# Key transfers spread over half cells, and probabilities of two cells added on GpSimd before the ones product, in a four-sublayer fp32 block on one core

## The chip, the core and the metric

One core of a Trainium2 chip runs the whole program: TensorE (PE) for matmuls, VectorE (DVE), ScalarE (ACT), GpSimd (POOL), and SyncE (SP), which issues nearly all DMAs. Each engine works through its own list in order and waits on semaphores. The metric is the device time of one execution in microseconds (us).

## What is computed

2048 tokens of width 128 pass six residual sublayers. All but the last but one are finished or nearly finished before the stage that matters here; that one is causal attention with 16 heads, softmax and a Gelu:

```
def _L1_attn_ref(x, Wk, bk, Wv, bv, Wf, bf):   # D_MODEL = 128, N_HEADS = 16, D_HIDDEN = 512
    Q = _split_heads(x, H)
    K = _split_heads(x @ Wk + bk, H)
    V = _split_heads(x @ Wv + bv, H)
    causal = jnp.tril(jnp.ones((S, S), dtype=bool))
    mask = jnp.where(causal, 0.0, -jnp.inf).astype(x.dtype)
    scores = jnp.einsum('bhqd,bhkd->bhqk', Q, K) + mask
    attn = jax.nn.softmax(scores, axis=-1)
    o = jnp.einsum('bhqk,bhkd->bhqd', attn, V)
    o = o.transpose(0, 2, 1, 3).reshape(B, S, -1)
    return x + jax.nn.gelu(o, approximate=False) @ Wf + bf
...
x = L0_attn_src                                # (1, 2048, 128)
x = x + 0.5 * _L0_ffn_ref(_layernorm(x, axis=-1), ...)      # 4-bit quantised
x = x + _L0_attn_ref(_layernorm(x, axis=-1), ...)           # linear attention
x = x + 0.5 * _L0_ffn_ref(_layernorm(x, axis=-1), ...)
x = x + 0.5 * _L1_ffn_ref(_layernorm(x, axis=-1), ...)      # relu
x = x + _L1_attn_ref(_layernorm(x, axis=-1), ...)           # the causal stage
x = x + 0.5 * _L1_ffn_ref(_layernorm(x, axis=-1), ...)
```

## The kernel before, in words

One list, PLAN, gives the order of all steps, and `follow` lets every engine walk it and emit its own part of each step. So the order in the plan is the order on each engine. The causal stage is built by `causal`.

Queries are cut into 4 chunks of 512, heads into 4 sets of 4 (two pairs of heads, pp = 0 and 1): 16 groups g, with chunk g // 4. A cell (g, kb) is one block of 128 keys against the 512 queries of the group's chunk; a group of chunk c has 4(c+1) cells, the last four on the diagonal and so narrower: 160 cells, numbered u. Group 8 begins with cell 48, group 12 with cell 96, group 15 with cell 144. A cell has two half cells i = 0, 1, one for each pair of heads. In half cell 0 of cell u PE makes `scores` of the first pair of heads (L1652), mostly one matmul pair `max` of a later group's row maxima (L1617), and `values` of cell u-1 (L1676: probabilities times V); in half cell 1 the other `scores`, another `max`, and `sums` of cell u-1 (L1691: a matrix of ones times the probabilities, which gives the softmax denominators). The remaining steps of a cell (transposes, output projection `wf`, the relu sublayer's `d_hidden`, `d_out`, keys and values of later chunks) stand behind the values, or, the second half of them, behind the sums.

ACT turns scores into probabilities `pr` (L966), a ring of 3 buffers of one cell each. DVE reduces each max matmul (L1289). Scores, max matmuls and most other PE outputs rotate through three PSUM sets in plan order, so a scores matmul reuses the set of the max matmul two before it, and a max matmul that of the scores in the half cell before. `row_max` (L1299 to L1303, three DVE instructions) gathers a group's maxima and splits them into two bf16 parts; PE turns them (`turn_max`, L1635), ACT copies them (L974), SP stores them into two rows of the queries (L653), where the group's first scores need them.

The denominators of a finished group go: ACT copy `take_d` (L987), gather by SP (L662), reciprocal on DVE (`invert`, L1307, two cells after the group's end), store (L669), spread to all rows (L676), product with the output on GpSimd (`norm`, L802, four cells after).

Keys and queries reach the tensors KK and QS through DRAM: GpSimd splits them into three bf16 parts (`split`, L792 to L795), SP stores these (`store_parts`, L626) and then issues 12 loads of 8 rows into KK (L634) and 12 into QS (L644), 64 KB each, one after the other. For chunk c these stand two groups before its first group, at the end of that group's maxima. `e_norm` and `d_norm` are layer norms' last step (L1088, DVE), after GpSimd's power (`rstd`, L696).

## Time and profile before

| | |
|---|---|
| median of 3 runs | 1105.21 us (1094.06 to 1112.79) |
| profiled execution | 1099.85 us |
| its span, first to last instruction | 1098.0 us |
| causal cells, from the first scores to the last exponential | 438 to 1067 us |
| mean granted TensorE clock | 0.944 of full speed |

A span is what the trace covers; what lies around it is 1.85 us. Each engine's busy time counts its instructions alone. A row of the timeline has start, duration, engine, line, operation, out<-in and count, and in brackets how long the engine had been idle and what released it. PE is TensorE, DVE VectorE, ACT ScalarE, POOL GpSimd, SPq the queue of SyncE.

### The profile page before, as it was taken

The page shows a single profiled execution, that of the slowest core. Times are in us where ns is not written, and L with a number is a line of the kernel's source. Part 1 is how long each engine was busy: PE and PEld are TensorE (multiplying, and loading weights), DVE is VectorE, ACT ScalarE, POOL GpSimd, SP SyncE. Part 2 cuts the span into 40 slices and gives each one's busy share as a digit, 9 for nine tenths or more (in the row PEclk, how much of TensorE's full clock was granted, in tenths as well). Part 3 has the DMA queues.
Part 4 walks back from the last instruction along what each step waited for, and adds up shares of the span by engine and source line. Part 5 has one row for each costly group of instructions (what it writes and reads, how often), then busy time and mean ns, then how long its engine had stood idle before and what let it go on. Part 6 is the DMA issues. An engine that isn't in the chain of part 4 may idle for free.

```text
span 1098.0 us, 19966 instructions
## 1 busy us (share of the span) xinstructions
PE 909.0 (83%) x7332; PEld 452.2 (41%) x7353; DVE 708.6 (65%) x1675; ACT 511.9 (47%) x884; POOL 257.4 (23%) x405
## 2 busy tenths in 40 slices
PE   2678887788888767928889699899899989999986
PEld 1444445666676655404334333243322223332225
DVE  7899953367887765638655487665579747677003
ACT  1133333243444323513565455656456656666763
POOL 1545420044555644204221001112000000000000
PEclk9899998898999987968999899899999989999998
DMA  5200000000000040050001400000400000000000
...
DMA packets 30935, 23.20 MB, mean 21 GB/s; under 512 B 9609, under 2 KB 27897, under 8 KB 30840
## 3 DMA queue, kind: packets, MB, share of 16 engines
...
q8 instruction: 61, 1.00, 0.4%
q10 hardware_dynamic: 912, 0.54, 0.2%
...
## 4 chain that ended last, share of the span: by engine, by line
PE 55%; DVE 18%; ACT 6%; POOL 6%; issue 6%; DMA 4%; SPq 4%; ACTq 0%; DVEq 0%; POOLq 0%
PE psum L1676 10%; PE psum L1691 10%; PE psum L1652 6%; PE psum L1617 5%; DVE arena L1289 4%; PE psum L1564 3%; PE psum L1533 2%; ACT arena L966 2%; POOL rs L696 2%; PE psum L1575 2%; DMA arena<-arena 2%; PE psum L1411 2%; PE psum L1370 2%; PE psum L1598 2%; PE psum L1705 2%
## 5 line engine op out<-in xcount | busy, mean ns | idle before, releaser
L1289 DVE TENSOR_REDUCE arena<-psum 128x2 f32<-128x1024 f32 (+2 forms) x320 | 335.6, 1063 | 154.1 <-PE psum L1617 95.7
L966 ACT ACTIVATE arena<-psum 128x1024 f32<-128x1024 f32 (+3 forms) x320 | 286.5, 897 | 157.1 <-PE psum L1652 90.7
L696 POOL TENSOR_TENSOR rs<-ve,mhalf 128x1 f32<-128x1 f32 x128 | 70.8, 559 | 397.1 <-DVE ve L1083 396.8
L1676 PE MATMUL psum<-arena 128*32 128x512 f32 (+3 forms) x1280 | 153.9, 554 | 1.3 <-ACT arena L966 1.3
L1691 PE MATMUL psum<-arena,ones 128*32 128x512 f32 (+3 forms) x1280 | 154.4, 555 | 0.0
L1617 PE MATMUL psum<-arena 48*128 48x512 bf16 (+3 forms) x640 | 113.5, 359 | 48.3 <-DMA arena<-scr_parts 20.6
L1652 PE MATMUL psum<-arena 50*128 50x512 bf16 (+3 forms) x640 | 116.9, 361 | 9.5 <-ACT arena L966 4.5
L1652 PEld LDWEIGHTS psum<-arena 50*128 50x128 bf16 x640 | 31.3, 93 | 203.8 <-issue 137.9
L802 POOL TENSOR_TENSOR arena<-arena 128x512 f32<-128x512 f32 x15 | 19.1, 1276 | 212.0 <-DMA arena<-scr_sums 212.0
L935 ACT ACTIVATE rh<-psum,fb 128x128 f32<-128x128 f32 x128 | 36.4, 369 | 66.1 <-PE psum L1564 63.2
L1617 PEld LDWEIGHTS psum<-arena 48*128 48x128 bf16 x640 | 35.9, 94 | 65.2 <-issue 26.2
L1370 PE MATMUL psum<-WguT,xqT 128*128 128x352 f32 x128 | 50.4, 522 | 7.7 <-DVE hb L1114 6.8
L1564 PE MATMUL psum<-xdT,fW 128*128 128x128 f32 x256 | 40.7, 309 | 16.4 <-DVE arena L1289 13.3
L1564 PEld LDWEIGHTS psum<-xdT,fW 128*128 128x128 f32 x256 | 35.7, 215 | 27.0 <-issue 22.5
L700 POOL TENSOR_TENSOR xv<-xv,xm 128x128 f32<-128x128 f32 x32 | 20.2, 631 | 112.4 <-DVE xv L1041 112.4
L1676 PEld LDWEIGHTS psum<-arena 128*32 128x32 f32 x1280 | 25.4, 109 | 40.8 <-issue 35.6
L1337 PE MATMUL psum<-bias_rows,onesb 128*128 128x128 bf16 (+1 forms) x107 | 28.5, 266 | 12.6 <-ACT arena L995 4.3
L854 ACT ACTIVATE th<-psum 128x352 f32<-128x352 f32 x32 | 14.8, 463 | 51.0 <-PE psum L1370 50.9
L1461 PE MATMUL psum<-arena 128*128 128x256 f32 x128 | 38.2, 397 | 0.0
L1575 PE MATMUL psum<-fW,rh 128*128 128x128 f32 x256 | 37.2, 291 | 0.0
L700 POOL TENSOR_TENSOR hv<-hv,hm 128x352 f32<-128x352 f32 x32 | 29.7, 930 | 29.8 <-DVE hv L1041 29.8
L1691 PEld LDWEIGHTS psum<-arena,ones 128*32 128x32 f32 x1280 | 25.5, 109 | 26.1 <-issue 21.4
...
## 6 DMA issues: line engine op xcount, KB each, us to landing
...
```

Source lines behind the costliest of these rows:

```text
L696: v.tensor_tensor(rs[:, u, t:t + 1], ve[:, u, t:t + 1], mhalf[:, :], ALU.pow).then_inc(s_rstd[u], 1)
L700: k = me.did(v.tensor_tensor(x, x, m, ALU.subtract))
L966: v.activation(pr[:, u % RING, pp, :, 0:CH - off], both(("scores", n))[0][:, :, off:CH], ACT.Exp).then_inc(s_p, 1)
L1289: v.tensor_reduce(MXP[:, j, 2 * pp:2 * pp + 2, m], both(("max", g, pp, j, m))[0][:, :, 0:hi - lo], AX_X, ALU.max).then_inc(s_mxd, 1)
L1370: last = mm(bank(b + k)[:, 0:GI], xqT[:, n % 2, :], WguT[:, k, :], start=True, stop=True)
L1461: last = mm(o, Wq[:, P * j:P * j + P], XNT[:, GRP * g:GRP * g + GRP], start=False, stop=True, skip_group_check=True)
L1564: last = mm(bank(b)[:, P * j:P * j + P], fW1[:, P * j:P * j + P], xdT[:, n % 2, :], start=True, stop=True)
L1575: last = mm(bank(b)[:, P:2 * P], rh[:, n % 2, j, :], fW2[:, j, :], start=False, stop=(j == FJ - 1), skip_group_check=True)
L1617: last = mm(o[:, par, 0:w], QS[c % 2][r, hp, P * j:P * j + P], KK[m][r, hp, 0:w], start=True, stop=(m < c), skip_group_check=True)
L1652: last = mm(o[:, par, off:CH], KK[kb // TPC][r, hp, P * (kb % TPC):P * (kb % TPC) + P], QS[c % 2][r, hp, off:CH], start=True, stop=(kb < T ...
L1676: last = mm(bank(O_BANK)[VD * h:VD * h + VD, off:CH], V[kb // TPC][:, kb % TPC, GH * (g % GPC) + h, :], pr[:, u % RING, h // 2, h % 2, 0:C ...
L1691: last = mm(bank(D_BANK)[VD * h:VD * h + VD, off:CH], ones1[:, 0:VD], pr[:, u % RING, h // 2, h % 2, 0:CH - off], start=(kb == 0), stop=en ...
```

## The change

In chunks 2 and 3 the full (not diagonal) cells of a group are taken in pairs (a, a+1), 40 pairs in all. GpSimd adds the probabilities of a+1 into those of a, in four instructions of 128 x 2 x 256 (`add_probs`: two halves of the queries, two pairs of heads), placed two and three cells after a. The ones product then runs over the sum, 256 queries at a time, in cells a+4 and a+5. The ring has 5 buffers (even cells use three, odd ones two), and exponentials wait for the products or additions that free theirs. The ones products of other cells stay one cell behind.

The 24 row loads of a chunk are issued two per half cell, queries and keys and the two row halves by turns, each pair once a given number of score matmuls is done. Chunk 1's store moves from half cell 10 to half cell 4. Reciprocals and norms come one cell later, Gelu one cell later and group by group, with the group outputs in a ring of 6. Maxima of groups 9 to 15 end one cell earlier. `e_norm` and `d_norm` of the causal stage and the two splitting instructions of `row_max` move from DVE to GpSimd. Some tensors of early stages now share their memory with the denominators.

```
-NORM_AT, GELU_AT = 4, 7
+PAIRED_FROM = 2
+ADD_AT, SUM_AT = 2, 4
+INVERT_AT, NORM_AT, GELU_AT = 3, 5, 8
+HELD = 6
+HALF = 256
...
-MAX_LEADS = {1: 2, 2: 3, 3: 3, 4: 3}
+MAX_LEADS = {1: 2, 2: 3, 3: 3, 4: 3, **{g: 5 for g in range(9, 16)}}
...
-        RING = 3
+        RING = 5
         pr = ce([RING, GP, 2, CH])
-        GT = [ce([GPC, CH]), ce([GPC, CH])]
-        DN = [ce([CH]), ce([CH])]
+        GT = ce([HELD, CH])
...
+        PAIRED = [a for g in range(MGROUPS) if g // GPC >= PAIRED_FROM
+                  for a in range(GROUP_U[g], GROUP_U[g + 1] - TPC, 2)]
+        SUMS = sorted([(a + SUM_AT + half, a, half) for a in PAIRED for half in range(2)]
+                      + [(a + 1, a, None) for a in range(len(CELLS))
+                         if a not in PAIRED and a - 1 not in PAIRED])
+        SUM_N = {(a, half): n for n, (_, a, half) in enumerate(SUMS)}
+        FIRST_SUM = {CELLS[a][0]: (a, half) for _, a, half in reversed(SUMS)}
+        LAST_SUM = {CELLS[a][0]: (a, half) for _, a, half in SUMS}
...
+        def slot(u):
+            return u // 2 % 3 if u % 2 == 0 else 3 + u // 2 % 2
...
-                if g % GPC == GPC - 2 and g + 2 < MGROUPS:
-                    slots[max_end[g]] += [("store_parts", g // GPC + 1), ("load_queries", g // GPC + 1)]
+            load_slot = {1: SECOND_KEYS_START + 4 * SECOND_KEYS_EVERY + 1, 2: max_end[6], 3: max_end[10]}
+            for c, first in load_slot.items():
+                slots.setdefault(first, []).append(("store_parts", c))
+                for k in range(4 * COMBOS):
+                    slots.setdefault(first + 1 + k // 2, []).append(("load_rows", c, k, first + 1 + k // 2))
...
-                    put(end + 2, "invert", g)
-                    put(end + 2, "store_inverse", g)
-                    put(end + 3, "spread_inverse", g)
+                    put(end + INVERT_AT, "invert", g)
+                    put(end + INVERT_AT, "store_inverse", g)
+                    put(end + INVERT_AT + 1, "spread_inverse", g)
                     put(end + NORM_AT, "norm", g)
...
+            for n, a in enumerate(PAIRED):
+                for k in range(2 * GP):
+                    put(a + ADD_AT + k // GP, "add_probs", 2 * GP * n + k)
...
+                    for when, a, half in SUMS:
+                        if (i, u) == (1, when):
+                            out.append(("sums", a, half))
+                            if LAST_SUM[CELLS[a][0]] == (a, half):
+                                out.append(("take_d", CELLS[a][0]))
...
+        POOL_NORMS = {x for x in PLAN[main:] if x[0] in ("d_norm", "e_norm")}
...
+            def load_rows(c, k, after):
+                par, n, keys = k % 2, k // 4, k // 2 % 2
+                if k == 0:
+                    sp.wait_ge(s_ptd, 48 * (c + 1))
+                    sp.wait_ge(s_att, c + 1)
+                    if c >= 2:
+                        sp.wait_ge(s_st, GP * GROUP_U[GPC * (c - 1)])
+                if after > 0:
+                    sp.wait_ge(s_st, after)
+                rows = slice(64 * par + QD * n, 64 * par + QD * n + QD)
+                part = scr[K_PART[n], 1] if keys else scr[Q_PART[n], 0]
+                src = part.rearrange("(a b r) s -> b r a s", b=2, r=QD)[par, :, :, CH * c:CH * c + CH]
+                if keys:
+                    sp.dma_start(KK[c][rows, :, :], src).then_inc(s_kk[c], 16)
+                else:
+                    sp.dma_start(QS[c % 2][rows, :, :], src).then_inc(s_qs[c % 2], 16)
...
+            def add_probs(n):
+                a, half, pp = PAIRED[n // (2 * GP)], n // GP % 2, n % GP
+                q = slice(HALF * half, HALF * half + HALF)
+                into = pr[:, slot(a), pp, :, q]
+                pool.wait_ge(s_av, a + 1)
+                pool.wait_ge(s_p, GP * (a + 1) + pp + 1)
+                v.tensor_tensor(into, into, pr[:, slot(a + 1), pp, :, q], ALU.add).then_inc(s_ps, 1)
+            def normed(u, n, t, y):
+                pool.wait_ge(s_rstd[u], n)
+                return v.tensor_scalar(y, X[:, t, :], mv[:, u, t, 0:1], rs[:, u, t:t + 1], ALU.subtract, ALU.mult)
+            def d_norm(n):
+                if ("d_norm", n) in POOL_NORMS:
+                    pool.wait_ge(s_xdt, n - TILES - 1)
+                    normed(4, n - TILES + 1, tile(n), xd[:, n % 2, :]).then_inc(s_xd, 1)
+            def row_max_parts(g):
+                pool.wait_ge(s_mxr, g + 1)
+                k = me.did(v.tensor_copy(MXH, MXS[:, :, :, 0]))
+                me.wait(k)
+                v.tensor_tensor(MXS[:, :, :, 1], MXS[:, :, :, 0], MXH, ALU.subtract).then_inc(s_mxn, 1)
...
-                if u >= RING:
-                    act.wait_ge(s_dn, u - RING + 1)
-                v.activation(pr[:, u % RING, pp, :, 0:CH - off], both(("scores", n))[0][:, :, off:CH], ACT.Exp
+                old = u - (4 if u % 2 else 6)
+                if old in PAIRED:
+                    act.wait_ge(s_dn, SUM_N[old, 1] + 1)
+                elif old - 1 in PAIRED:
+                    act.wait_ge(s_ps, 2 * GP * (PAIRED.index(old - 1) + 1))
+                    act.wait_ge(s_av, old + 1)
+                elif old >= 0:
+                    act.wait_ge(s_dn, SUM_N[old, None] + 1)
+                v.activation(pr[:, slot(u), pp, :, 0:CH - off], both(("scores", n))[0][:, :, off:CH], ACT.Exp
...
-                k = me.did(v.tensor_reduce(MXS[:, :, :, 0], MXP[:, :, :, 0:c + 1], AX_X, ALU.max, negate=True))
-                me.wait(k)
-                k = me.did(v.tensor_copy(MXH, MXS[:, :, :, 0]))
-                me.wait(k)
-                v.tensor_tensor(MXS[:, :, :, 1], MXS[:, :, :, 0], MXH, ALU.subtract).then_inc(s_mxn, 1)
+                v.tensor_reduce(MXS[:, :, :, 0], MXP[:, :, :, 0:c + 1], AX_X, ALU.max, negate=True).then_inc(s_mxr, 1)
...
-            def sums(u):
+            def sums(u, half):
                 g, kb = CELLS[u]
-                c = g // GPC
-                off = P * max(kb - TPC * c, 0)
-                end = kb == TPC * (c + 1) - 1
-                if kb == 0:
+                off = P * max(kb - TPC * (g // GPC), 0)
+                lo, hi = (off, CH) if half is None else (HALF * half, HALF * half + HALF)
+                first, end = FIRST_SUM[g] == (u, half), LAST_SUM[g] == (u, half)
+                if first:
                     B[D_BANK].free(pe)
+                if half is None:
+                    pe.wait_ge(s_p, GP * (u + 1))
+                else:
+                    pe.wait_ge(s_ps, 2 * GP * PAIRED.index(u) + GP * (half + 1))
                 for h in range(GH):
-                    last = mm(bank(D_BANK)[VD * h:VD * h + VD, off:CH], ones1[:, 0:VD],
-                              pr[:, u % RING, h // 2, h % 2, 0:CH - off], start=(kb == 0), stop=end,
+                    last = mm(bank(D_BANK)[VD * h:VD * h + VD, lo:hi], ones1[:, 0:VD],
+                              pr[:, slot(u), h // 2, h % 2, lo - off:hi - off], start=first, stop=end,
                               skip_group_check=True)
                 last.then_inc(s_dn, 1)
```

How this lies on the engines. PE early in group 13 (before), two half cells: scores, maxima, values, then scores, maxima (with a mask) and the sums of 512 columns.

```order
L1652 MATMUL psum<-arena 128x512 x2
L1617 MATMUL psum<-arena 128x512 x2
L1676 MATMUL psum<-arena 32x512 x4
L1652 MATMUL psum<-arena 128x512 x2
L1617 MATMUL psum<-arena 128x384 x2
L1623 MATMUL psum<-ident,mask_kq 128x64 x4
L1691 MATMUL psum<-arena,ones 32x512 x4
```

The same place of the kernel after: L1723 are the scores, L1688 the maxima, L1747 the values, L1408 and L1646 the relu sublayer's `d_out`, L1694 a mask, L1766 the sums.

```order
L1723 MATMUL psum<-arena 128x512 x2
L1688 MATMUL psum<-arena 128x512 x2
L1747 MATMUL psum<-arena 32x512 x4
L1408 MATMUL psum<-bias_rows,onesb 128x128
L1646 MATMUL psum<-fW,rh 128x128 x4
L1723 MATMUL psum<-arena 128x512 x2
L1688 MATMUL psum<-arena 128x128 x2
L1694 MATMUL psum<-ident,mask_kq 128x64 x4
L1766 MATMUL psum<-arena,ones 32x256 x4
L1723 MATMUL psum<-arena 128x512 x2
```

The sums have 256 columns in place of 512; in the group's cells 1 to 3 none stand, in its diagonal cells one more than before.

SP around chunk 3's reload (before): L626 stores, L634 and L644 are the loads, L662 gathers, L653 stores maxima.

```order
L653 DMA arena<-arena 2x512 x4
L626 DMA scr_parts<-arena 128x2x512 x3
L634 DMA arena<-scr_parts 8x8x512 x12
L644 DMA arena<-scr_parts 8x8x512 x12
L683 DMA out_dram<-X 128x128 x2
L662 DMA arena<-arena 32x1x16 x4
L669 DMA scr_sums<-arena 128x16
L676 DMA arena<-scr_sums 32x512 x4
```

The first load of chunk 1 and what follows it on SP (after): L659 stores, L676 and L678 load keys and queries, L696 gathers, L687 stores maxima, L703 and L710 store and spread the inverse.

```order
L687 DMA arena<-arena 2x512 x8
L659 DMA scr_parts<-arena 128x2x512 x3
L678 DMA arena<-scr_parts 8x8x512 x2
L676 DMA arena<-scr_parts 8x8x512 x2
L678 DMA arena<-scr_parts 8x8x512 x2
L676 DMA arena<-scr_parts 8x8x512 x2
L696 DMA arena<-early 32x1x16 x4
L678 DMA arena<-scr_parts 8x8x512 x2
L687 DMA arena<-arena 2x512 x4
...
L703 DMA scr_sums<-arena 128x16
L678 DMA arena<-scr_parts 8x8x512 x2
L710 DMA early<-scr_sums 32x512 x4
```

Gathers, stores of maxima and the inverse's two transfers now stand between the loads, and the loads of keys and queries alternate.

GpSimd near the end of the stage (after), where before nothing but L802 (here L864) and powers stood: L842 are the additions, L855 and L857 the two splitting instructions of the row maxima.

```order
L842 TENSOR_TENSOR arena<-arena 128x2x256 x12
L864 TENSOR_TENSOR arena<-arena,early 128x512
L842 TENSOR_TENSOR arena<-arena 128x2x256 x4
L855 CAST arena<-arena 128x16
L857 TENSOR_TENSOR arena<-arena 128x16
L842 TENSOR_TENSOR arena<-arena 128x2x256 x12
```

The splitting of a group's maxima waits behind the additions that stand ahead of it.

## Rows read from the trace of the kernel before

**Rows 1.** The page's first part: busy us, share of the span, instructions
```profile
PE 909.0 (83%) x7332; PEld 452.2 (41%) x7353; DVE 708.6 (65%) x1675; ACT 511.9 (47%) x884; POOL 257.4 (23%) x405
```

**Rows 2.** Windows of the three reloads: columns in the first row
```profile
core 0: us, PE busy (x) PEld busy (x) DVE busy (x) ACT busy (x) POOL busy (x), PEclk, DMA share, GB/s
472.00:492.00 20.00, 0.00 (x0) 0.00 (x0) 2.04 (x6) 0.88 (x2) 0.00 (x0) 0.56 0.54 66
606.00:626.00 20.00, 13.42 (x138) 5.50 (x134) 8.00 (x12) 9.70 (x15) 0.55 (x1) 0.96 0.54 83
773.00:790.00 17.00, 14.74 (x154) 5.65 (x146) 9.72 (x13) 10.08 (x16) 0.55 (x1) 1.00 0.52 103
```

**Rows 3.** Timeline of SP around chunk 1's store: start, us, line, operation
```profile
450.70 2.42 SPq L653 DMA_DIRECT2D arena<-arena  x4
...
464.34 1.46 SPq L626 DMA_DIRECT2D scr_parts<-arena  x3
468.07 4.17 SPq L634 DMA_DIRECT2D arena<-scr_parts  x12
```

**Rows 4.** Timeline of PE over the first stall
```profile
471.34 0.22 PE L1659 MATMUL psum<-ident,mask_qk 64*128 64x64 bf16 x4
...
492.19 0.71 PE L1617 MATMUL psum<-arena 48*128 48x512 bf16 x4 [20.63 <-DMA arena<-scr_parts]
```

**Rows 5.** Timeline over the second stall: SP's gather, the reciprocal, PE
```profile
614.96 3.69 SPq L662 DMA_DIRECT2D arena<-arena  x4
...
627.52 0.25 DVE L1307 RECIPROCAL arena<-arena 128x16 f32<-128x16 f32 x1 [10.55 <-DMA arena<-arena]
...
628.73 2.05 PE L1564 MATMUL psum<-xdT,fW 128*128 128x128 f32 x8 [8.69 <-DVE arena L1289]
...
634.18 0.84 PE L1617 MATMUL psum<-arena 48*128 48x512 bf16 x4
```

**Rows 6.** Timeline of PE after the third stall
```profile
792.96 2.05 PE L1564 MATMUL psum<-xdT,fW 128*128 128x128 f32 x8 [4.63 <-DVE arena L1289]
```

**Rows 7.** Timeline of PE over one cell of group 12
```profile
880.25 0.39 PE L1652 MATMUL psum<-arena 50*128 50x512 bf16 x2
...
880.48 0.38 PE L1617 MATMUL psum<-arena 48*128 48x512 bf16 x2
...
880.79 1.06 PE L1676 MATMUL psum<-arena 128*32 128x512 f32 x8
...
881.79 0.39 PE L1652 MATMUL psum<-arena 50*128 50x512 bf16 x2
...
883.32 0.39 PE L1652 MATMUL psum<-arena 50*128 50x512 bf16 x2
```

**Rows 8.** Timeline of PE and ACT where a half cell is short
```profile
924.85 0.39 PE L1652 MATMUL psum<-arena 50*128 50x512 bf16 x2
...
925.28 1.02 ACT L966 ACTIVATE arena<-psum 128x1024 f32<-128x1024 f32 x1 [0.61 <-PE psum L1652]
...
926.45 0.39 PE L1617 MATMUL psum<-arena 48*128 48x512 bf16 x2 [0.31 <-ACT arena L966]
```

**Rows 9.** Timeline of PE in group 15, two score matmuls
```profile
1034.23 0.39 PE L1652 MATMUL psum<-arena 50*128 50x512 bf16 x2
...
1035.55 0.39 PE L1652 MATMUL psum<-arena 50*128 50x512 bf16 x2
```

**Rows 10.** Timeline of PE: a ones product of 256 columns on a diagonal cell
```profile
530.81 0.64 PE L1691 MATMUL psum<-arena,ones 128*32 128x256 f32 x8
531.38 0.39 PE L1652 MATMUL psum<-arena 50*128 50x512 bf16 x2
```

**Rows 11.** Line L802, GpSimd's product: duration ns min/median/max, first and last start
```profile
L802 POOL TENSOR_TENSOR arena<-arena x15: 1256/1272/1327, 495.8 to 1038.4; 128x512 f32<-128x512 f32 x15
```

**Rows 12.** Waits from 438 to 690: us in total, times, longest
```profile
PE psum L1617 <- DVE arena L1289: 6.7, 13, 1.6
```

89 lines of the change are left out of this document (44 added, 45 removed).

## Prediction

> **What bounds the kernel now.** I read the page's engine totals first [rows 1]: PE is busy 83% of the span, DVE 65%, GpSimd (POOL) 23%. An average over stages says little, so I then followed the score matmuls (L1652) and exponentials (L966) cell by cell along the timeline, from 438 us, where the causal stage begins, to its end at 1068. Everything before is untouched by the edits. Two pictures come out.
>
> In undisturbed cells PE is never idle. The reader should see four blocks that repeat [rows 7]: scores 880.25, row-maximum scores 880.48, values 880.79, the next scores 881.79, and after the ones product (sums) the next cell's scores at 883.32. That is 3.07 us a cell: twice (0.54 of scores and maxima + 0.99 of values or sums). Group 15 has no maxima left to make; there a half cell takes 1.32 [rows 9], so 2.64 a cell.
>
> Between them lie stalls. The largest: PE's last matmul before 471.6, the next at 492.19, waiting 20.63 for the reload of keys and queries [rows 4]. A second: PE waits 8.69 to 628.73, because DVE's reciprocal of the denominators (L1307) sat 10.55 waiting for its gather, which SP could issue only after 24 row loads (614.96 to 618.65) and which then queued behind them; DVE's maxima, and PE with them, stood behind that reciprocal [rows 5]. A third of the same kind: 4.63 to 792.96 [rows 6]. The remaining idle times of several us are the Gelu blocks on ACT, which the change leaves where they are, one cell later.
>
> **Spreading the row loads.** Chunk 1. Now its store is issued at 464.34, behind the maxima of group 2, and the loads run from 468.07 to 492.2, 24.1 us for 24 [rows 3, 4]. After, it stands right behind the maxima of group 1, issued by 453.12 (450.70 + 2.42). With the same 3.73 from store to first load, the loads start at 456.9 and end at 480.9, if the queue works at the same rate; the issue gates (score matmuls 5 to 16) open before that, since the 16th is passed at about 469. PE arrives at 471.6, so it waits 9.3 instead of 20.6: 11.3 saved. Bounds: the chunk-3 loads move 103 GB/s against 66 here [rows 2]; at that rate they end near 472 and about 18 are saved. The last pair now stands behind the spread of group 0's inverse on SP, which can cost 3: 8 saved. I take 11.5.
>
> Chunk 2. The gather is now issued after 16 to 20 loads and the reciprocal one cell later, so I expect the 8.69 to go. But the queue was busy throughout 606 to 626 [rows 2], so the last load still lands near 626.5. The first maximum that needs it stands 5.4 behind the end of the present stall (628.73 to 634.18 [rows 5], at the low clock); PE would be there at about 620.0 + 4.5 = 624.5 and wait 2. That leaves 6.7, plus about 2 because less runs at the low clock: in [rows 2] the granted clock is 0.56 in the stall without any matmul. I take 8.5, between 5 (the wait moves) and 11.5. Chunk 3: the first user is four cells later, nothing new waits; 4.6 plus some 2.4 of low clock, 7 (4.6 to 8).
>
> What the row loads are limited by is a matter of its own: the DMA share is 0.54, 0.54 and 0.52 while they run [rows 2], about half of the 16 engines, whatever PE does. The Trainium skill (DMA: Bandwidth & Descriptors, the section on why a DMA adds 16 to its semaphore) says that a transfer uses the largest number of engines up to 16 that divides the slowest dimension of both sides; these have 8 rows, so 8 engines, and the trace agrees with that half. By that rule issuing them apart gains no rate, only an earlier start, and the sum above, which keeps the present rate, is the one that follows; a sum in which spreading doubled the rate would save all of the first stall.
>
> **Pairing.** 80 full cells of chunks 2 and 3 become 40 pairs. Each pair drops one ones product of 512 columns (two halves of 256 remain). A 512-column product holds PE for 0.99; one of 256 columns from 530.81 to 531.38, 0.57 [rows 7, 10]. PE's work falls by 40 x 2 x (0.99 - 0.57) = 34 us. This is the gain that the diff seems to promise. I don't book it, because of what is late next. A half cell without a long product shows it already: scores at 924.85, their exponential 925.28 to 926.30, and the next half cell's maxima matmul at 926.45, after 0.31 idle, since it writes the PSUM set that this exponential reads [rows 8]. So from a score matmul to the maxima matmul of the next half cell at least 1.60 pass. Today it takes 1.53 + 0.23 = 1.76, no wait. With the sums half at 1.11, or at 0.54 where no sums stand, PE waits until 1.60, then makes the maxima (0.31) and values (0.99): 2.90 a cell, 0.17 less than 3.07. Group 15 has no maxima, but its values need the same exponential: 1.60 + 0.99 = 2.59 against 2.64. The delayed half products also fall on diagonal cells, which are short and PE bound: three of 0.57, 1.7 a group. So per group 8 or 12 x 0.17 saved and 1.7 lost; over groups 8 to 14 about nothing, in group 15 a loss of 1: together +1.5 (bounds: -34 if the chain does not bind, +6).
>
> **GpSimd.** Each pair costs it four additions of 512 elements a partition. The nearest row is its product of the same size, 1.27 [rows 11]; with 0.07 between instructions 5.36 a pair, 2.68 a cell against 2.90 on PE. It fits, by 8%. An addition may run late by about 4.8 us before the exponential that reuses the odd buffer waits (all four done 7.3 after the cell a+1 starts, needed at about 12). The other work, key splits in groups 8 and 9, fits into that slack but not far: +1. New on the path: the split of the row maximum now sits behind two additions; the additions of that cell end 1.5 us into it, cast and subtraction some 0.6, while PE's transpose comes at 1.8: about 0.4 to 0.5, up to 1.3, in seven groups, +3 (0 to 9). The norms moved off DVE save it 0.34 each; PE waits for DVE's maxima 6.7 between 438 and 690 [rows 12], of which I take 3 (0 to 7). At the tail four GpSimd powers now precede the first norm: +0.5.
>
> **Sum.** -11.5 - 8.5 - 7 - 3 + 1.5 + 1 + 3 + 0.5 = -24. The profiled execution took 1099.85 (span 1098.0 and 1.85 around it), hence 1075.9; it lies 5.4 below the median shown, 1105.21, whose runs go from 1094 to 1113. From the median: 1081.
>
> **Rivals.**
> 1. Pairing pays in full. For it: PE is busy almost throughout chunks 2 and 3. Against: [rows 8], where 0.31 of wait appears as soon as a half cell is short. Time: 1081 - 34 = 1047. Chance 0.2.
> 2. The loads come no earlier, since SP works in order and the last pair waits behind a spread, or PE meets them later with the same wait: the first two stalls keep their length. 1081 + 20 = 1101. Chance 0.17.
> 3. Slower: GpSimd becomes the pace. It decides at 5.8 us a pair, that is at 1.38 an addition instead of 1.27. If access in two pieces and port conflicts make it 1.9, a pair takes 7.9 and 40 pairs cost 40 x 2.1 = 84 minus what the diagonals give back (a third): 1081 + 55 = 1136. For it: nothing else has so little room. Against: all 15 products lie between 1.256 and 1.327 [rows 11], with DVE busy beside them. Chance 0.15.
> 4. The forecast: 1081, own range 1065 to 1095. Chance 0.48.
>
> **Numbers.** A measurement of this kernel tells about 2% from no change; that is 1083 here, just above the forecast. So faster takes all of rival 1 (0.2) and some 0.6 of the forecast's 0.48 (0.3); same the other 0.18 and rival 2 (0.17); slower rival 3. The range 1046 to 1104 leaves out most of rival 3 and little else.
>
> **What would show it.** Right: PE's wait for row loads near 480 under 12 us; the reciprocals' wait for the gather near zero; cells of group 14 at 2.85 to 2.95 with a wait of 0.2 to 0.3 for L966 before the maxima; group 15 at 2.6; additions at 1.27. Wrong: cells of 2.65 in group 14 (rival 1), PE waiting for GpSimd before its sums (rival 3), an unchanged first stall (rival 2). The forecast falls above all if the short half cell does not wait.

## The result and the profile after

| | before | after |
|---|---|---|
| median of 20 runs | 1102.31 us (1094.06 to 1112.79) | 1090.73 us (1086.8 to 1100.3) |
| ratio, 95% interval | | 0.9914 [0.9886, 0.9942] |
| profiled execution | 1099.85 us | 1090.75 us |
| its span | 1098.0 us | 1088.9 us |
| last exponential, then to the end | 1067.0, 31.0 us | 1052.8, 36.1 us |
| mean granted clock | 0.944 | 0.945 |

By the ratio, which goes by means, the change makes the kernel 9.5 us faster (0.9%; the medians are 11.6 apart), within the 2% that the prediction called no change. The forecast was 24. The direction and the range held; the size was 2.1 to 2.5 times too large. Below, an execution that the record marks as slow is left out of medians and ratios: one of no_pairs_tail (1087.58 us) and one of no_pairs_once (4405.95 us).

The page's totals of the kernel after answer to [rows 1]:

```profile
PE 892.8 (82%) x7353; PEld 456.9 (42%) x7353; DVE 694.3 (64%) x1609; ACT 509.6 (47%) x887; POOL 489.2 (45%) x631
```

The windows from the first exponential of group 8 (680.2 and 659.3) to the last one, first of the kernel before, then of the kernel after (columns as in [rows 2]):

```profile
680.00:1067.00 387.00, 365.22 (x3360) 117.09 (x3360) 230.56 (x286) 242.07 (x311) 28.75 (x41) 0.97 0.06 15
```

```profile
659.00:1053.00 394.00, 344.28 (x3358) 119.71 (x3357) 224.15 (x259) 239.43 (x311) 239.03 (x227) 0.96 0.06 15
```

These two rows hold the case. PE works 21 us less in chunks 2 and 3 (the prediction had counted 34), and the stretch is 7 us longer, while GpSimd goes from 29 us of work to 239. What the kernel gained, it gained ahead of group 8: that group starts at 659.3 in place of 680.2, 20.9 earlier. From there on 6.8 are given back up to the last exponential, and 5.1 in the tail.

PE's waits from 438 us on, after (us in total, times, longest):

```profile
PE psum L1688 <- ACT arena L1034: 22.1, 41, 4.1
PE psum L1688 <- DMA arena<-scr_parts: 12.3, 1, 12.3
PE psum L1706 <- POOL arena L857: 10.5, 5, 5.1
...
PE psum L1625 <- POOL xd L846: 5.4, 5, 4.2
```

The first line is the chain of the prediction (maxima behind exponentials, 41 times; one of these waits, 4.1, stands behind a Gelu block). The second is the first stall, 12.3 in place of 20.63 [rows 4]. The other two are new: PE's transposes wait for GpSimd's row-maximum split (L857) and for its layer norms (L846).

The same stretches side by side, one profiled execution each, measured from the first exponential of a group to that of the next (us). The kernels between are those of the experiments below:

```
                 g2    g6    g8    g9    g10   g11-14 g15   tail
before           40.1  42.2  49.6  47.5  48.3  201.1  40.3  31.0
after            31.2  32.0  53.4  50.2  44.4  201.4  44.1  36.1
loads_only       26.3  39.1  49.6  47.5  49.1  200.5  40.3  32.1
loads_invert     31.8  40.9  48.3  47.9  41.6  201.5  40.3  31.0
no_pairs         30.5  31.3  48.0  48.1  41.8  200.9  40.3  35.2
tiny_adds        29.4  31.9  48.0  48.0  41.6  199.4  44.2  35.5
norms_dve        29.6  32.3  51.0  49.7  44.0  199.6  41.7  33.5
half_exps        29.2  34.4  52.5  50.5  44.0  187.5  34.7  34.2
tail_early2      29.7  31.3  47.9  48.1  41.8  200.6  40.3  30.9
```

### The profile page after: what moved, and what is told of

It is laid out like the page before. It is cut to its first block, busy times and chain, and to the rows that moved or that the text cites. A ratio compares the mean times of both kernels' runs of the same rounds, so it can differ in the third digit from the quotient of the medians.

```text
span 1088.9 us, 20340 instructions
## 1 busy us (share of the span) xinstructions
PE 892.8 (82%) x7353; PEld 456.9 (42%) x7353; DVE 694.3 (64%) x1609; ACT 509.6 (47%) x887; POOL 489.2 (45%) x631
## 4 chain that ended last, share of the span: by engine, by line
PE 50%; DVE 14%; POOL 12%; ACT 10%; issue 7%; DMA 4%; SPq 2%; ACTq 0%; POOLq 0%; DVEq 0%
PE psum L1747 9%; PE psum L1766 6%; ACT arena L1034 6%; PE psum L1723 5%; DVE arena L1364 5%; POOL arena L842 4%; PE psum L1688 4%; PE psum L1482 3%; PE psum L1635 2%; PE psum L1441 2%; POOL rs L730 2%; PE psum L1492 2%; PE psum L1646 2%; PE psum L1604 2%; PE psum L1408 2%
## 5 line engine op out<-in xcount | busy, mean ns | idle before, releaser
L842 POOL TENSOR_TENSOR arena<-arena 128x512 f32<-128x512 f32 x160 | 199.3, 1273 | 82.2 <-PE psum L1747 54.5
L1747 PE MATMUL psum<-arena 128*32 128x512 f32 (+3 forms) x1280 | 157.7, 566 | 5.8 <-ACT arena L1034 5.8
L1688 PE MATMUL psum<-arena 48*128 48x512 bf16 (+3 forms) x640 | 112.7, 354 | 53.4 <-ACT arena L1034 22.1
L1723 PE MATMUL psum<-arena 50*128 50x512 bf16 (+3 forms) x640 | 117.1, 364 | 12.2 <-ACT arena L1034 4.9
L1766 PE MATMUL psum<-arena,ones 128*32 128x256 f32 (+3 forms) x1280 | 113.3, 440 | 0.0
L1723 PEld LDWEIGHTS psum<-arena 50*128 50x128 bf16 x640 | 31.4, 93 | 171.5 <-issue 90.5
L1688 PEld LDWEIGHTS psum<-arena 48*128 48x128 bf16 x640 | 35.3, 94 | 83.0 <-ACT arena L1034 40.2
L1408 PE MATMUL psum<-bias_rows,onesb 128*128 128x128 bf16 (+1 forms) x128 | 38.1, 298 | 13.3 <-ACT arena L1064 4.2
L1747 PEld LDWEIGHTS psum<-arena 128*32 128x32 f32 x1280 | 25.7, 109 | 42.2 <-issue 30.1
L1635 PEld LDWEIGHTS psum<-xdT,fW 128*128 128x128 f32 x256 | 35.3, 213 | 12.4 <-issue 7.8
L1766 PEld LDWEIGHTS psum<-arena,ones 128*32 128x32 f32 x1280 | 28.0, 109 | 25.7 <-issue 15.8
L1646 PE MATMUL psum<-fW,rh 128*128 128x128 f32 x256 | 38.3, 296 | 0.0
```

The source lines that it names most:

```text
L842: v.tensor_tensor(into, into, pr[:, slot(a + 1), pp, :, q], ALU.add).then_inc(s_ps, 1)
L1408: mm(o, onesb[:, 0:P], bias_rows[:, at:at + n], start=start, stop=False, skip_group_check=True)
L1635: last = mm(bank(b)[:, P * j:P * j + P], fW1[:, P * j:P * j + P], xdT[:, n % 2, :], start=True, stop=True)
L1646: last = mm(bank(b)[:, P:2 * P], rh[:, n % 2, j, :], fW2[:, j, :], start=False, stop=(j == FJ - 1), skip_group_check=True)
L1688: last = mm(o[:, par, 0:w], QS[c % 2][r, hp, P * j:P * j + P], KK[m][r, hp, 0:w], start=True, stop=(m < c), skip_group_check=True)
L1723: last = mm(o[:, par, off:CH], KK[kb // TPC][r, hp, P * (kb % TPC):P * (kb % TPC) + P], QS[c % 2][r, hp, off:CH], start=True, stop=(kb < T ...
```

## Experiments

### Which part brings the gain, and which loses it

**loads_only.** The kernel before, with `load_rows` in place of the 24 loads in a row, and chunk 1's store earlier.

```
+            load_slot = {1: SECOND_KEYS_START + 4 * SECOND_KEYS_EVERY + 1, 2: max_end[6], 3: max_end[10]}
+            for c, first in load_slot.items():
+                slots.setdefault(first, []).append(("store_parts", c))
+                for k in range(4 * COMBOS):
+                    slots.setdefault(first + 1 + k // 2, []).append(("load_rows", c, k, first + 1 + k // 2))
```

> The kernel before with one part of the change alone: store of chunk 1 earlier and the 24 row loads of each chunk issued in pairs behind score matmuls; no pairing, no moved norms, splits or reciprocals. Theory Q (what is missing of the forecast was lost behind GpSimd's in-order list: row-maximum splits, norms, and the low clock that their waits bring): the loads bring nearly all that they were forecast to, about 20 us off the kernel before, with chunk 2's stall only partly gone because the reciprocal still stands one cell earlier: ratio 0.978 to 0.985, PE's wait near 480 at 12 to 13 us. Theory L (the loads themselves bring less than forecast): ratio 0.988 to 0.995, like the whole change. Theory P (the pairing gives the gain back) expects the same as Q here.

1085.28 us (6 runs), ratio 0.985 [0.9803, 0.9896], at the upper edge of what theory Q gave. So the loads alone already bring 17 us of the median, more than the whole change. PE's wait for the rows is 6.4, not the 12 to 13 expected, since PE comes to it later; groups 0 to 2 together take 62.7 in place of 70.7. But cells 35 and 75, the stalls of chunks 2 and 3, are still 12.4 and 12.1 long: there the reciprocal stands where it stood.

**loads_invert.** The same, with the reciprocal and what follows it (store, spread, norm, Gelu) one cell later.

```
-                    put(end + 2, "invert", g)
+                    put(end + 3, "invert", g)
```

> The loads alone (as in the run loads_only, whose cell 35 still took 12.4 us and cell 75 12.1), with reciprocal, store, spread and norm of each group one cell later and Gelu one cell later, as in the change. If the stalls of chunks 2 and 3 come from the reciprocal that stands too early behind row loads, cells 35 and 75 fall to 4.3 and 4.7 as in the changed kernel, and 7 to 14 us go: 1071 to 1078, ratio to before 0.970 to 0.980. If the moved loads or the maxima's lead did it, they stay above 10 and the time at 1084.

1079.18 us (4 runs), ratio 0.9791 [0.9737, 0.9845]. The reciprocal does it: cell 75 falls from 12.1 to 4.1 and group 10 from 49.1 to 41.6. Cell 35 falls to 4.28 as well, but in this execution PE waits 7.6 for the rows themselves a cell later; more on that below. Spread loads and later reciprocals together bring 23 us, close to the 27 that the prediction gave to the three stalls. The median lies 1 above the range expected.

**no_pairs.** The whole change but the pairing.

```
-PAIRED_FROM = 2
+PAIRED_FROM = 4
```

> The changed kernel without the pairing: no additions on GpSimd, every ones product over 512 columns one cell behind; all else stays, norms and row-maximum splits on GpSimd too. Theory Q: GpSimd's list is nearly empty in chunks 2 and 3, so the waits for the splits (10.5 us, 5 times in the changed kernel) go; full cells go back from 2.90 to 3.07 and diagonals get shorter, which nearly cancels; the tail keeps its norms on GpSimd. Some 8 to 14 us under the changed kernel, 1075 to 1082 in one profile. Theory P: also lower, by what the pairing costs in group 15 (cells of 3.6 at the low clock, 4 us) and in the diagonals. Theory L: same as the changed kernel, within 3 us.

1079.18 us (6 runs), ratio 0.9788 [0.9733, 0.9842], an interval that lies wholly below the changed kernel's. So the pairing costs some 11 us. The median is that of loads_invert, though the tail is 4 longer (35.2 for 31.0): ahead of the tail the norms and splits on GpSimd, without additions beside them, cost nothing, and may bring some us. The maxima of groups 9 to 15, one cell earlier here and not in loads_invert, show nothing: groups 9 to 14 take 290.8 and 291.0. Groups 8 to 10 take 10.1 us less than in the changed kernel, group 15 3.8 less.

### Where the pairing loses it

**tiny_adds.** Additions of 8 columns in place of 256.

```
-                into = pr[:, slot(a), pp, :, q]
+                into = pr[:, slot(a), pp, :, HALF * half:HALF * half + 8]
```

> The changed kernel with the same 160 additions at the same places, each over 8 columns for each head instead of 256, so the sums of denominators lack most of the second cell's probabilities; everything waits for the same events. GpSimd loses some 190 us of work while PE, ACT and DVE keep theirs. Theory Q: the splits and norms come at once, PE's waits for GpSimd fall from 19 us to the tail's 4, and the kernel takes 1076 to 1082. Theory P: the pairing's cost lies on PE and ACT (half cells without a long product wait for the exponential), not on GpSimd: 1086 to 1090. In both, group 14's cells stay at 2.90, since nothing of the chain from scores through the exponential to the next matmul is touched; if they fall to 2.65, GpSimd's work had slowed the exponentials or maxima.

1080.12 us (6 runs), ratio 0.9789 [0.9748, 0.9831]. With the additions' work gone, the paired kernel is as fast as the one without pairing (1079.18). On PE, ACT and DVE the pairing is thus worth nothing that the runs can tell (by their intervals the two ratios may lie 0.7% apart either way), as forecast. What the pairing loses comes with the length of the additions: 10.6 us by the medians, 14 by the ratios, give or take 6. Group 14's cells stay at 2.92.

Between the profiles of tiny_adds and the changed kernel nearly all of it lies in three places, the last full cell of groups 8, 9 and 10, where the next group's maxima are split and turned. Cell 55 takes 14.1 in place of 8.4, cell 67 7.2 in place of 5.1, cells 79 and 80 together 10.5 in place of 7.7.

What that time does is seen in cell 55, ahead of group 9. GpSimd in the changed kernel:

```profile
678.93 1.27 POOL L864 TENSOR_TENSOR arena<-arena,early 128x512 f32<-128x512 f32 x1
680.16 2.50 POOL L842 TENSOR_TENSOR arena<-arena 128x512 f32<-128x512 f32 x2
682.65 0.80 POOL L846 TENSOR_SCALAR xe<-X,mv,rs 128x128 f32<-128x128 f32 x1
683.53 0.45 POOL L820 TENSOR_TENSOR X<-X,xe 128x128 f32<-128x128 f32 x1
683.94 2.48 POOL L842 TENSOR_TENSOR arena<-arena 128x512 f32<-128x512 f32 x2
686.37 0.20 POOL L855 CAST arena<-arena 128x16 bf16<-128x16 f32 x1
686.65 0.22 POOL L857 TENSOR_TENSOR arena<-arena 128x16 f32<-128x16 f32 x1
```

DVE and PE of the same execution:

```profile
680.59 0.20 DVE L1374 TENSOR_REDUCE arena<-arena 128x16 f32<-128x48 f32 x1
```

```profile
681.54 0.33 PE L1655 MATMUL psum<-ident,xe 128*128 128x128 f32 x1
686.92 1.02 PE L1706 MATMUL psum<-ident,arena 128*8 128x128 f32 x4 [5.05 <-POOL arena L857]
687.87 0.60 PE L1723 MATMUL psum<-arena 50*128 50x512 bf16 x2
```

DVE has the row maxima ready at 680.8, but GpSimd's cast of them begins at 686.37, behind a product, four additions, a norm and its add: 7.5 us without a gap. The split needs 0.5 us of work and comes 5.6 us late; PE's transpose (L1706) waits 5.05. Then the clock is at its lower level (0.50 granted from 687 to 692): the four transposes take 1.02, and 0.60 below. The same place in no_pairs, GpSimd and PE:

```profile
678.05 0.45 POOL L820 TENSOR_TENSOR X<-X,xe 128x128 f32<-128x128 f32 x1
679.93 0.20 POOL L855 CAST arena<-arena 128x16 bf16<-128x16 f32 x1 [1.43 <-DVE arena L1374]
```

```profile
680.83 0.33 PE L1655 MATMUL psum<-ident,xe 128*128 128x128 f32 x1
680.99 0.60 PE L1706 MATMUL psum<-ident,arena 128*8 128x128 f32 x4
```

There GpSimd is idle when the maxima arrive, and PE doesn't wait.

**both_dve, rowmax_dve, norms_dve.** The neighbours of the additions back on DVE: splits and norms, the splits alone, the norms alone.

The norms (both_dve, norms_dve), and the splits (both_dve, rowmax_dve; `row_max` on DVE is again that of the kernel before):

```
-        POOL_NORMS = {x for x in PLAN[main:] if x[0] in ("d_norm", "e_norm")}
+        POOL_NORMS = set()
...
             def row_max_parts(g):
-                pool.wait_ge(s_mxr, g + 1)
-                k = me.did(v.tensor_copy(MXH, MXS[:, :, :, 0]))
-                me.wait(k)
-                v.tensor_tensor(MXS[:, :, :, 1], MXS[:, :, :, 0], MXH, ALU.subtract).then_inc(s_mxn, 1)
+                return
```

> The changed kernel with pairing and loads, but the layer norms' last step and the two splitting instructions of the row maximum back on DVE. Theory Q: PE's wait for L857's split disappears (it was 10.5 us, 5.05 of it before group 9 at 681.9), as does that for the norms (8.7), and the low-clock stretch behind each; the tail is 3 us shorter. Expected 1074 to 1080 in one profile, ratio to before 0.975 to 0.985. Theory P: only the tail's 3 us and little more, 1084 to 1088, ratio 0.987 to 0.992. DVE, busy 65% of the time, may give up to 4 us of that back in either case.

> The changed kernel with only the two splitting instructions of the row maximum back on DVE; norms stay on GpSimd. Both together brought 6 us (1084.4), of which the tail's norms should be 3. Theory Q: the wait of turn_max for GpSimd (10.5 us in the profile) turns into one for DVE of 1 to 3; 4 to 8 us less than the changed kernel, 1083 to 1087, ratio 0.982 to 0.988. If the splits are not what PE waits for in the end, since the norms queued beside them on GpSimd hold the next step too: within 2 us of the changed kernel, 1089 to 1092.

> The changed kernel with only the 20 last steps of layer norms back on DVE; the row-maximum splits stay on GpSimd behind the additions. The tail's share is 3 us (four norms at 0.78 one after the other on GpSimd against 0.30 on DVE). In group 8, where the split waited 5.05 behind two pairs of additions and a norm with its add, 0.8 less stands ahead of it. Theory Q: 1086 to 1088, ratio 0.984 to 0.989, that is the tail and 1 to 2 more. If norms on GpSimd are the main loss (PE's d_turn waited 8.7 for them in the profile, 4.2 of it in the tail): 1083 to 1085.

both_dve 1084.37 (0.9844 [0.9795, 0.9892]), rowmax_dve 1088.43 (0.9895 [0.9854, 0.9935]), norms_dve 1081.9 (0.9836 [0.9794, 0.9877]). The splits alone bring 2 us, nearer to the second expectation than to the first; the norms alone 9, more than either theory's number, of which the tail has 2.6 in the profiles (33.5 against 36.1). In norms_dve the wait before group 9 is 2.90 in place of 5.05, and the total:

```profile
PE psum L1706 <- POOL arena L857: 6.8, 6, 2.9
```

Each of the three intervals is wide against these differences (0.5%, 5 us), and both_dve isn't below norms_dve, so the three don't divide the loss exactly between splits and norms. both_dve, for which theory Q had 1074 to 1080, came out at theory P's 1084 to 1088. All keep groups 8 to 10 longer than no_pairs: 145.2 in both_dve and 137.9 there, though no split and no norm stands on GpSimd any more.

One reason is in both_dve's trace. The split of cell 67 on GpSimd, DVE and PE:

```profile
743.23 4.95 POOL L842 TENSOR_TENSOR arena<-arena 128x512 f32<-128x512 f32 x4
```

```profile
746.12 0.86 DVE L1371 CAST arena<-arena 128x16 bf16<-128x16 f32 x1
747.01 1.19 DVE L1373 TENSOR_TENSOR arena<-arena 128x16 f32<-128x16 f32 x1
```

```profile
748.26 0.60 PE L1705 MATMUL psum<-ident,arena 128*8 128x128 f32 x4 [0.88 <-DVE arena L1373]
```

The cast and the subtraction take 0.17 and 0.18 on DVE where no addition runs beside them; here 0.86 and 1.19. In both_dve and rowmax_dve 19 of these steps in chunks 2 and 3 took more than 0.2, up to 1.27, and every one of them ended 0.03 after one of GpSimd's additions. The norms on DVE are lengthened too (0.34, up to 1.42), the maxima's reductions of 1.23 aren't. So moving the small steps off GpSimd doesn't take them out of the additions' way. How much of both_dve's loss this is, no run shows; its transposes wait 2.4 in all for the subtraction.

**adds_last.** The additions behind a cell's other steps, not ahead of them.

```
-                out += [x for x in here if x[0] in ("gelu", "add_probs")]
+                out += [x for x in here if x[0] == "gelu"]
...
+                out += [x for x in here if x[0] == "add_probs"]
```

> The changed kernel with its pairing, with one thing moved: in GpSimd's list the additions of a cell stand behind that cell's other steps instead of ahead of them. Theory Q (what the pairing loses, 11 us between no_pairs and the changed kernel, is lost by splits, norms and key parts that stand behind 2.5 us of additions): the row-maximum splits come 2.5 us earlier, the 5.05 wait before group 9 shrinks by 2 to 3, the others go, and the kernel takes 5 to 8 us less than the changed one: 1083 to 1086, ratio 0.982 to 0.987. Rival H (a step at the head that waits for another engine now holds the additions back, and the sums with them): PE waits for GpSimd before its sums, 1090 to 1096.

1091.04 us (7 runs), ratio 0.9911 [0.9873, 0.9949]: the same as the changed kernel. My expectation of 5 to 8 us fell, and so did the rival of waits before the sums. PE's wait before group 9 is 4.03 and the sum of such waits 9.6. What is late is not one step behind the additions of its own cell: ahead of the split GpSimd works from 675.56 to 689.0 without a gap, so the list as a whole runs late there. Its order within a cell doesn't help.

**plain_early2, paired_early2, chunk3_early2.** Three kernels with all norms on DVE and the loads of chunk 2 earlier (tail_early2, below), without pairing, with it, and with pairing in chunk 3 alone (`PAIRED_FROM` 4, 2, 3).

> No pairing, all 20 moved layer norms back on DVE, keys and loads of chunk 2 three cells earlier. Against the run tail_early2 (1070.3), which keeps 16 of them on GpSimd: 16 x 0.34 of DVE work in the early chunks, of which little is on the path. Expected 1069 to 1074, ratio 0.970 to 0.976, tail 31.

> The same with the pairing of chunks 2 and 3. If the loss is one of neighbours on GpSimd (norms above all), only the row-maximum splits are left behind the additions and the loss against plain_early2 is 3 us or less: 1070 to 1076. If it is the additions' own, it is what the traces of norms_dve showed against no_pairs in groups 8 to 10, 3.0 + 1.6 + 2.2, and up to 2 in group 15: 6 to 9 us more than plain_early2, 1077 to 1081. If pairing pays once everything beside it is cleared, it would be below plain_early2; nothing so far speaks for that.

> The same with the pairing of chunk 3 only, where GpSimd has no key splits and few norms beside the additions. By the traces groups 12 to 14 then take 59.0, 57.6 and 45.6 as in norms_dve, against 60.6, 57.6 and 45.8 without pairing, and group 15 39.5 to 44.1 against 40.3, by whether a slice of low clock falls into it: between 2 us less and 3 us more than plain_early2, the same within the measurement.

1074.38 (0.9755 [0.9713, 0.9797]), 1078.54 (0.9803 [0.9757, 0.9849]) and 1071.71 (0.973 [0.9683, 0.9776]). With the norms cleared away, the pairing costs 4 in the medians, between the two sizes expected (3 or less, 6 to 9), and every one of the six paired runs (1075.94 to 1086.45) is longer than every one of the six without (1071.84 to 1075.72). The profiles show 5.7 between the start of group 8 and the last exponential (384.6 against 378.9), and groups 8 to 10 lose 6.6 (3.5, 1.6, 1.5), where key parts and splits stand on GpSimd. In chunk 3 alone it costs nothing and brings nothing that these runs can tell. So the additions have a price where GpSimd has other work on the path, and in chunk 3 neither a price nor a return that shows.

### Why PE's 21 us don't count

**half_exps.** Exponentials of chunks 2 and 3 over half their columns.

```
-                v.activation(pr[:, slot(u), pp, :, 0:CH - off], both(("scores", n))[0][:, :, off:CH], ACT.Exp
+                hi = CH - off if u < GROUP_U[8] else (CH - off) // 2
+                v.activation(pr[:, slot(u), pp, :, 0:hi], both(("scores", n))[0][:, :, off:off + hi], ACT.Exp
```

> The changed kernel, with every exponential of chunks 2 and 3 over the first half of its columns only, so that half of the probabilities there are stale values. Nothing else changes in any list. If the chain from the scores through the 1.02 us exponential to the next half cell's maxima (which write the same PSUM set) holds the paired cells at 2.92 against 2.65 of PE's own work, as the prediction had it, group 14's full cells fall to 2.65 to 2.70 and group 15's from 2.51 to 2.0 to 2.2. If GpSimd or DVE holds them, both stay within 0.05 of what they are: GpSimd's four additions take 5.0 to 5.3 a pair, so no cell under 2.55 on the mean can last, and group 15 may stay at 2.5 for that reason.

1067.64 us (one run). Group 14's cells fall from 2.92 to 2.64, group 15's from 2.51 to 2.21, with the additions as long as before. PE in group 14, first of the changed kernel:

```profile
975.65 0.39 PE L1723 MATMUL psum<-arena 50*128 50x512 bf16 x2
...
976.66 0.39 PE L1723 MATMUL psum<-arena 50*128 50x512 bf16 x2
977.25 0.39 PE L1688 MATMUL psum<-arena 48*128 48x512 bf16 x2 [0.20 <-ACT arena L1034]
```

and of half_exps (its lines are numbered one higher: L1724 scores, L1689 maxima, L1748 values):

```profile
976.00 0.39 PE L1724 MATMUL psum<-arena 50*128 50x512 bf16 x2
...
977.12 0.39 PE L1724 MATMUL psum<-arena 50*128 50x512 bf16 x2
977.35 0.38 PE L1689 MATMUL psum<-arena 48*128 48x512 bf16 x2
977.66 1.06 PE L1748 MATMUL psum<-arena 128*32 128x512 f32 x8
978.65 0.39 PE L1724 MATMUL psum<-arena 50*128 50x512 bf16 x2
```

In the changed kernel the maxima at 977.25 come 1.60 after the scores of the half cell before (975.65), exactly the 1.60 of [rows 8], with 0.20 of wait. With the short exponential the same matmul (977.35) comes 1.35 after the scores of the half cell before (976.00) and 0.23 after its own, where it was 0.59, and waits for nothing. The chain through the exponential and the PSUM set is what holds a paired cell, shown by shortening it. Even then groups 8 and 9, with GpSimd's late steps, stay at 52.5 and 50.5.

### The loads and the tail

**no_pairs_once.** No pairing, and chunk 1's 24 loads all at once behind the store.

```
-                    slots.setdefault(first + 1 + k // 2, []).append(("load_rows", c, k, first + 1 + k // 2))
+                    at_slot = first + 1 + (k // 2 if c > 1 else 0)
+                    slots.setdefault(at_slot, []).append(("load_rows", c, k, at_slot if c > 1 else 0))
```

> The changed kernel without pairing, as in the run no_pairs, and with all 24 row loads of chunk 1 issued at once, right behind its store. In three versions that spread them PE starts again at 482.9 to 483.8, 3.5 after the last pair was issued behind the spread of group 0's inverse (478 to 480). Theory S (the last pair's place behind that spread sets the end): issued at 455 to 463, the loads end when the queue is through with them, near 478 to 480, and PE's wait shrinks by 3 to 5 us. Theory R (the rate of 8 of 16 engines sets it, 24 us for 24 loads from 456.9): they end at 481, 2 to 3 us earlier at most, and the maxima of group 2 and the gather of group 0, now behind all 24, come later by up to 8: no gain or a loss of up to 3.

1084.36 us (3 runs), ratio 0.9843 [0.9767, 0.992]: 5.2 over no_pairs, but the intervals overlap. The first stall moves to cell 7, which takes 16.6 in place of 2.7, because group 2's maxima now reach their rows behind all 24 loads. Groups 1 and 2 together take 49.1 in place of 44.6; theory R is nearer. Of the 9.2 between the two profiled executions (1082.56 and 1073.35) these groups have 4.5; another 4.6 lies ahead of the causal stage (first exponential at 440.5 and 435.9), where the two kernels are the same.

**no_pairs_tail.** No pairing, and the last four layer norms on DVE.

```
+        POOL_NORMS = {x for x in PLAN[main:] if x[0] in ("d_norm", "e_norm") and x[1] < 3 * TILES - TPC}
```

> The changed kernel without pairing, as in the run no_pairs, and with the last four layer norms of the tail back on DVE. The GpSimd norms are 0.78 apart and their first transpose waited 4.2 after 4 powers; on DVE it was 3.1, and 0.8 less for each following tile is hidden or not. Expected: tail from the last exponential 32 to 33 us instead of 35.2, so 2 to 3 us under no_pairs in a like run; ratio to before 0.973 to 0.979. If the tail's extra time is only a slice of low clock that falls elsewhere, it stays at 35 to 36.

1074.64 us (5 runs), ratio 0.9755 [0.9703, 0.9807]. The tail is 31.0 in the profile, as before the change, against 35.2: more than expected from the norms alone. The changed kernel's tail:

```profile
1067.86 0.44 PE L1625 MATMUL psum<-ident,xd 128*128 128x128 f32 x1 [4.23 <-POOL xd L846]
1068.64 0.47 PE L1625 MATMUL psum<-ident,xd 128*128 128x128 f32 x1 [0.34 <-POOL xd L846]
...
1082.65 2.02 PE L1646 MATMUL psum<-fW,rh 128*128 128x128 f32 x8
```

and the same two transposes and product in the kernel before:

```profile
1080.66 0.58 PE L1554 MATMUL psum<-ident,xd 128*128 128x128 f32 x2 [3.08 <-DVE xd L1088]
1081.43 0.65 PE L1554 MATMUL psum<-ident,xd 128*128 128x128 f32 x2 [0.19 <-DVE xd L1088]
...
1093.60 1.11 PE L1575 MATMUL psum<-fW,rh 128*128 128x128 f32 x8
```

The first transpose waits 4.23 for 3.08, and the product takes 2.02 for 1.11. Each norm is 0.80 on GpSimd, 0.34 on DVE, and the longer idle time is followed by more of the lower clock: 0.74 granted from 1068 to 1081 and 0.54 from there to 1089 after, 0.90 from 1082 to the end before.

**tail_early2.** no_pairs_tail, and chunk 2's keys, store and loads three cells earlier.

```
-                lo, hi = GROUP_U[GPC * (c - 2)] + KEYS_START[c], GROUP_U[GPC * c - 2] - MAX_LEAD
+                lo, hi = GROUP_U[GPC * (c - 2)] + KEYS_START[c], GROUP_U[GPC * c - 2] - MAX_LEAD - (3 if c == 2 else 0)
...
-            load_slot = {1: SECOND_KEYS_START + 4 * SECOND_KEYS_EVERY + 1, 2: max_end[6], 3: max_end[10]}
+            load_slot = {1: SECOND_KEYS_START + 4 * SECOND_KEYS_EVERY + 1, 2: max_end[6] - 6, 3: max_end[10]}
```

> No pairing and the tail's norms on DVE, as in the run no_pairs_tail, and besides the keys of chunk 2 made three cells earlier and their store and 24 row loads issued three cells (six half cells) earlier. In profiles of like lists PE's wait for these rows before cell 36 was 0.4, 0.9, 2.2, 2.5 and 4.8 us, with cell 36 between 5.6 and 11.9, as the packets took 0.076 to 0.093 us each: if that is the queue's own variation, nothing waits any more, cell 36 is at 5.2 to 5.6 in every run, 3 to 4 us go in the median (1072 to 1074, ratio 0.971 to 0.975) and the spread of the runs gets narrower than 1071 to 1088. If the earlier keys collide with the maxima and output steps of group 5, whose cells are already 5 to 7 us, the gain is eaten there: 1075 to 1078.

1070.31 us (6 runs, 1064.6 to 1073.1), ratio 0.9722 [0.9689, 0.9755]: the fastest version, 20 us under the changed kernel and 2 below what was expected. In all four profiles with this edit cell 36 takes 5.62 or 5.63, and PE waits for no row loads there. Without it, identical lists differed. The windows of the loads, no_pairs and then no_pairs_tail, whose plans are the same up to the tail and whose first load of chunk 2 is issued at 591.7 and 591.8:

```profile
592.00:608.00 16.00, 15.37 (x167) 6.30 (x162) 11.14 (x15) 10.70 (x17) 2.63 (x3) 1.00 0.56 100
608.00:620.00 12.00, 11.52 (x123) 5.02 (x122) 8.20 (x14) 6.25 (x11) 1.78 (x4) 1.00 0.15 33
```

```profile
592.00:608.00 16.00, 15.38 (x165) 6.73 (x158) 10.84 (x14) 10.09 (x16) 2.63 (x3) 1.00 0.58 84
608.00:620.00 12.00, 7.25 (x49) 3.21 (x48) 4.46 (x9) 3.01 (x6) 1.53 (x4) 0.72 0.28 39
```

and PE's wait for the rows, 0.4 and 4.8:

```profile
PE psum L1688 <- DMA arena<-scr_parts: 0.4, 1, 0.4
```

```profile
PE psum L1688 <- DMA arena<-scr_parts: 4.8, 1, 4.8
```

The DMA engines' shares are alike (0.56, 0.58), but 100 GB/s are moved in one execution and 84 in the other. PE then idles, the granted clock of the second window is 0.72 on the mean, and group 6 takes 31.3 or 37.6. Why the same transfers are slower in one execution isn't settled.

## The prediction, point by point

**First stall: −11.5 forecast, −8.3 found.** PE waits 12.33 in place of 20.63 [rows 4], and group 2 is 8.9 shorter. The bound of 8 was the right one, and the reason that it gave fits. SP after:

```profile
470.41 0.67 SPq L678 DMA_DIRECT2D arena<-scr_parts  x2
478.55 1.71 SPq L710 DMA_DIRECT2D early<-scr_sums  x4
480.30 0.67 SPq L676 DMA_DIRECT2D arena<-scr_parts  x2
```

The last pair stands behind the spread of group 0's inverse, and PE starts again 3.5 later, at 483.79. In no_pairs and both_dve it is 3.5 after the last pair too (480.43 and 482.85), in loads_only 5.1 (483.0). From the first load's issue to PE's start pass 26.8, in no_pairs 26.0, in both_dve 23.1, against 24.1 before: the place behind the spread costs up to 3 and the queue's rate sets the rest. No run moves that place alone. (The other bound, about 18, should have been 20 by the prediction's own figures: 20.6 of wait less 0.7.) By the rule of the Trainium skill (DMA: Bandwidth & Descriptors, on why a DMA adds 16 to its semaphore) a load of 8 rows runs on 8 of the 16 engines, whenever it is issued. The DMA share while such loads run is 0.56 and 0.58 in the windows above, and the trace agrees. But a share is no rate: 84 and 100 GB/s were moved at it.

**Chunk 2: −8.5 forecast; −10.2 in the profile.** The mechanism held: L1378 waits for no gather there, and cell 35 falls from 15.54 to 4.28. The price depends on the execution: in the nine other profiles of the changed kernel's versions that keep this part as it is, group 6 took 31.3, 31.5, 31.9, 32.3, 32.4, 34.4, 37.5, 37.6 and 37.6, against 32.0 in the changed kernel's, and in loads_invert 40.9. The one profile of the prediction couldn't show such a spread, and neither the 2 us of new wait nor the −10.2 found is a property of the change.

**Chunk 3: −7 forecast, −3.9 found, −6.5 without the pairing.** Group 10 took 48.3, then 44.4, and 41.8 in no_pairs. The stall went as said; the pairing took 2.6 of it.

**Pairing on PE: +1.5 forecast, about +1 found** (tiny_adds against no_pairs, 1080.12 and 1079.18, which the runs can't tell from nothing). The chain of 1.60 held to the hundredth, cells came out at 2.92 for 2.90, and rival 1 (1047) fell with it. Group 15's cells were 2.51 in place of 2.59. What wasn't foreseen is that the clock can fall to its lower level in them. Group 15 in the changed kernel:

```profile
1009.00:1013.00 4.00, 2.65 (x28) 0.63 (x24) 0.00 (x0) 3.83 (x6) 0.29 (x1) 1.00 0.01 1
1013.00:1027.00 14.00, 11.80 (x54) 1.58 (x54) 0.25 (x1) 7.60 (x8) 10.87 (x9) 0.51 0.06 20
```

PE idles 1.26 ahead of a matmul at 1011.31 and works 2.65 of the 4 us up to 1013; then the clock is at 0.51 of 2.4 GHz, the lower level, for 14 us, and cells take 3.59 in place of 2.51. Group 15 took 39.5, 41.7 or 44.1 (44.2 in tiny_adds) in paired kernels, by whether and how long this occurs, and 40.3 in every unpaired one. Why it occurs isn't shown: in both_dve, rowmax_dve, paired_early2 and chunk3_early2 PE does the same up to there, with the same idle times, and the clock stays at 1.00.

**GpSimd: +1 and +3 forecast, +10.6 found. This is the step that failed.** The addition was sized rightly, if a little long: [rows 11] said 1.27, four in a row take 4.95 (5.36 were counted), and the trace after gives

```profile
L842 POOL TENSOR_TENSOR arena<-arena x160: 1252/1272/1303, 665.0 to 1046.0; 128x512 f32<-128x512 f32 x160
```

so rival 3 (1136, from 1.38 on) was rightly turned down as a rate. But the prediction compared 5.36 with 5.8 a pair and let "the other work, key splits in groups 8 and 9" fit "into that slack but not far". It priced the row-maximum split behind the two additions of its own cell. Adding up one stretch of the list would have shown more: from 678.93, 5.0 for four additions, 1.27 for the product, 1.25 for a norm and its add are 7.5 us, against cells of 2.9 to 3.4. An engine that is 85% taken by one kind of work (4.95 of 5.84, two cells of 2.92) has little slack for the others, and the latest of them carried PE's next transpose. Nor did the prediction ask what the additions do to short steps on DVE: in the changed kernel those steps have left DVE, but both_dve shows that moving them back isn't free either. The true cost lay between the forecast and rival 3, which counted the lack of room only from the point where the additions alone don't fit.

**Norms off DVE: −3 forecast, wrong in sign beside the additions.** With them back on DVE the kernel is 9 faster (norms_dve). Without additions it isn't settled. tail_early2, with 16 of the 20 norms on GpSimd, lies 4 below plain_early2, with none (1070.31 and 1074.38), and no_pairs has the median of loads_invert in spite of a tail 4 longer. Both point the way that was forecast, but in each pair the intervals overlap, and the profiles of tail_early2 and plain_early2 differ by 0.3 between group 8 and the last exponential and by 1.4 in the tail. The waits of [rows 12], 6.7, hardly changed: 7.1 in the changed kernel, 7.9 with the norms back on DVE; without pairing 5.5 in tail_early2 and 6.2 in plain_early2.

**Tail: +0.5 forecast, +5.1 found.** Only the powers were counted, which stood there before too; the four norms in a row on GpSimd and the clock after them were not. (The tail is the end of the last relu sublayer, which runs beside and after the causal stage; other than the opening says, it isn't nearly finished before it.)

In sum: everything but the pairing gave 23 (no_pairs, its longer tail included) where 29.5 were forecast (27 for the stalls, 3 for the norms, less 0.5 in the tail), and the pairing took 11 where 5.5 were. That is −12, the −11.6 between the medians again: the two parts are cut at no_pairs, so their sum is no check of either.
